# Attention's last quotient moved into the next stage, one of that stage's loads moved into attention, and one early load cut in four

## The reference

```python
def _L1_attn_ref(x, Wq, Wk, Wv, Wo):
    ...
    q = (x @ Wq.T).reshape(B, T, H, Dh)          # H = 16, Dh = 16, T = 2048
    k = (x @ Wk.T).reshape(B, T, H, Dh)
    v = (x @ Wv.T).reshape(B, T, H, Dh)
    q = _apply_rotary(q, cos, sin)
    k = _apply_rotary(k, cos, sin)
    ...
    scores = jnp.einsum('bhqd,bhkd->bhqk', q, k) * scale
    scores = jnp.where(causal[None, None], -jnp.inf, scores)
    attn = jax.nn.softmax(scores, axis=-1).astype(v.dtype)
    out = jnp.einsum('bhqk,bhkd->bhqd', attn, v)
    out = out.transpose(0, 2, 1, 3).reshape(B, T, C)
    return out @ Wo.T
...
x = L0_attn_x
x = x + _L0_attn_ref(_layernorm(x, axis=-1), ...)
x = x + _L0_ffn_ref(_layernorm(x, axis=-1), ...)
x = x + _L1_attn_ref(_layernorm(x, axis=-1), L1_attn_Wq, L1_attn_Wk, L1_attn_Wv, L1_attn_Wo)
x = x + _L1_ffn_ref(_layernorm(x, axis=-1), L1_ffn_router_w, L1_ffn_expert_weights)
```

## Time and profile before

| | us |
|---|---|
| median of 3 runs | 2865.2 (2860.91 to 2867.78) |
| the profiled execution | 2864.33 |
| its span, first to last instruction | 2862.6 |
| around the span | 1.73 |
| project_qkv | from about 1022 to 1286 |
| attention | from 1291.8 to 2319.7 |
| tail | from 2319.7 to the end |

### The profile page before, as it was taken

One profiled execution on the slowest core, in us unless ns is written; L12 is line 12 of the kernel. 1 busy time (PEld: TensorE's weight loads), 2 busy tenths in 40 slices (PEclk: granted clock), 3 DMA queues, 4 the chain that ended last, 5 costly groups with the idle time before them and its releaser, 6 DMA issues. The chain is left out here.

```text
span 2862.6 us, 63267 instructions
## 1 busy us (share of the span) xinstructions
PE 2456.2 (86%) x24666; PEld 1415.1 (49%) x24666; DVE 1570.9 (55%) x2607; ACT 1793.6 (63%) x2682; POOL 735.8 (26%) x1006
## 2 busy tenths in 40 slices
PE   6888888886688889958999999999999977789872
PEld 3555555454567656633434333333333356567652
DVE  5767768577775467745454544445554337520133
ACT  3443535343565445438999999999999933356421
POOL 2203021120000036831212111112211103464465
PEclk9999999998799899978999999999999988799986
DMA  7800000000200024575656677665667234478767
GB/s 253 274 30 2 1 1 1 1 1 9 38 1 1 1 61 145 162 136 107 112 108 115 127 115 125 113 110 102 124 123 119 48 100 150 155 259 268 257 224 238
DMA packets 251996, 308.83 MB, mean 108 GB/s; under 512 B 100544, under 2 KB 180160, under 8 KB 251584
## 3 DMA queue, kind: packets, MB, share of 16 engines
q1 hardware_dynamic: 237344, 269.49, 40.0%
q0 software_dynamic: 12288, 33.57, 3.4%
q10 hardware_dynamic: 2080, 1.84, 0.2%
HBM read 157.23 MB, written 147.59 MB: 106 GB/s over the span
## 5 line engine op out<-in xcount | busy, mean ns | idle before, releaser
L1779 ACT ACTIVATE at_PT<-at_pS 128x1024 f32<-128x1024 f32 (+2 forms) x1152 | 1002.3, 1239 | 13.7 <-PE at_pS L1806 13.6
L1634 POOL TENSOR_SCALAR_AFFINE_SELECT at_PT<-at_PT 128x256 f32<-128x256 f32 (+1 forms) x384 | 197.4, 523 | 825.3 <-ACT at_PT L1779 824.8
L1806 PE MATMUL at_pS<-hd_QT,hd_KT 99*32 99x512 bf16 (+3 forms) x5120 | 316.4, 351 | 7.4 <-DVE at_QT L1751 4.8
L1806 PE MATMUL at_pS<-at_QT,at_KT 99*32 99x512 bf16 (+3 forms) x5120 | 317.6, 349 | 2.2 <-issue 0.8
L1727 DVE COPY at_OT<-at_pO 128x512 f32<-128x512 f32 x64 | 44.3, 692 | 478.8 <-PE at_pO L1824 473.8
L1824 PE MATMUL at_pO<-at_PT,at_V 128*32 128x512 f32 (+3 forms) x2560 | 290.4, 530 | 5.8 <-issue 5.6
L1824 PE MATMUL at_pO<-at_PT,hd_V 128*32 128x512 f32 (+3 forms) x2560 | 286.7, 530 | 0.0
L2369 PE MATMUL tl_bank<-tl_W,tl_xT 128*128 x896 | 238.1, 404 | 32.0 <-issue 29.6
L1806 PEld LDWEIGHTS at_pS<-at_QT,at_KT 99*32 99x32 bf16 x5120 | 117.7, 95 | 256.2 <-ACT at_PT L1779 166.9
L1806 PEld LDWEIGHTS at_pS<-hd_QT,hd_KT 99*32 99x32 bf16 x5120 | 111.7, 95 | 267.5 <-ACT at_PT L1779 171.2
L451 ACT ACTIVATE la_ft<-la_ft 128x1024 f32<-128x1024 f32 x128 | 135.1, 1056 | 161.2 <-DVE la_ft L274 161.0
(11 more groups left out here) (353 smaller groups left out, 4161.6 us busy)
## 6 DMA issues: line engine op xcount, KB each, us to landing
tl_xin<-rows_in SPq DMA_DIRECT2D x56, 512.0 KB
rows_out<-tl_yout SPq DMA_DIRECT2D x56, 512.0 KB
score_terms<-at_parts SPq DMA_DIRECT2D x60, 384.0 KB, 5.4
rows_in<-la_zeros SPq DMA_DIRECT2D x8, 2048.0 KB, 7.6
rotated_qk<-qk_qkT SPq DMA_DIRECT2D x16, 1024.0 KB, 4.3
at_qk<-rotated_qk SPq DMA_DIRECT2D x60, 256.0 KB, 4.3
rows_in<-la_zeros SPq DMA_DIRECT2D x4, 3072.0 KB, 11.3
values<-qk_rv SPq DMA_DIRECT2D x64, 192.0 KB, 4.6
```

Source lines behind the costliest of these rows:

```text
L1634: nc.gpsimd.affine_select(out=d, in_=d, compare_op=ALU.is_ge, fill=0.0, base=0, pattern=of, channel_multiplier=-1).then_inc(masked, 1)
L1779: nc.scalar.activation(PT[u % 6][:, 0:banks, 0:width], pS[u % 3][:, 0:banks, 0:width], ACT.Exp, scale=HD ** -0.5).then_inc(exp_done, 1)
L1806: last = mm(pS[u % 3][r:r + 32, b, col:col + 512 - off], KT[par][0:KS, h, kb * P + r:kb * P + r + 32], QT[par][0:KS, h, c * 512 + off:(c + ...
```

## The change

**Attention's end.** For the last chunk of the last group (it 15, c 3) `finish` stops after the copy to `OT`. The swap, reciprocal and product are in a new function `quotient`, which DVE calls in the tail behind add(2). `keep_out(15, 3)` is left out; the four stores stand in the tail, on SP, between the weights of step c = 2 and the load of chunk 3, behind a wait for the quotient (`last_divided`). The load of chunk 15, which needs them, waits for their landing (`last_stored`). `OT` and `aT1` now lie in the buffer `y0`, which the tail first uses for its products much later.

**Attention's middle.** The load of the tail's chunk 0 is issued by SP in attention, at the end of `it` = 3, into a buffer `ay0` of its own that outlives the stage. The tail's SP starts with a semaphore increment in its place, and then loads chunk 1.

**project_qkv.** The load of `V0` is cut into four loads of 192 KB, each behind one `qkT` store of batch 2; the wait for the stores of batch 0 goes before the first.

```diff
@@ project_qkv, SP
-            store(2)
+            def first_values(q):
+                if q == 0:
+                    for f in range(4):
+                        sp.wait_ge(v_stored[f], 16 + 16 * 4)
+                sp.dma_start(keep["V0"][:, 4 * q:4 * q + 4, :], keep["v"][0, 4 * q:4 * q + 4].rearrange("t p e -> p t e")).then_inc(first_out, 16)
+            store(2, first_values)
             sp.wait_ge(first_split, 4)
             sp.dma_start(keep["terms"][0].rearrange("s r n -> r s n"), first_parts).then_inc(first_out, 16)
...
-            sp.dma_start(keep["V0"][:, :, :], keep["v"][0].rearrange("t p e -> p t e")).then_inc(first_out, 16)
             def first_terms(q):
                 if q == 0:
-                    sp.wait_ge(first_out, 32)
+                    sp.wait_ge(first_out, 80)
@@ new
+def quotient(v, dve, out, sums):
+    v.stream_shuffle(out[:, :], sums[:, :], list(range(HD, 2 * HD)) + list(range(HD)))
+    dve.drain()
+    v.reciprocal(out[:, :], out[:, :])
+    dve.drain()
+    return v.tensor_tensor(out[:, :], sums[:, :], out[:, :], ALU.mult)
@@ attention, SP
-                keep_out(it, 3)
+                if more:
+                    keep_out(it, 3)
+                if it == 3:
+                    for k in range(2):
+                        sp.wait_ge(stored[k], 64 + 2 * 128)
+                    sp.dma_start(keep["ay0"][:, :, :], keep["ao"].rearrange("(b a) h e n -> b (a h e) n", a=G)[0, :, 0:512].rearrange("(c p) n -> p c n", p=P)).then_inc(tail_loaded, 16)
@@ attention, DVE
                 v.tensor_copy(OT[:, :], pO[s][:, :]).then_inc(out_copied, 1)
...
+                if (it, c) != (NIT - 1, QC - 1):
+                    dve.drain()
+                    quotient(v, dve, aT[s], OT).then_inc(divided, 1)
@@ tail, SP
-            for c in range(NT // 4):
+            sp.sem_inc(a_loaded[0], 16)
+            for c in range(1, NT // 4):
                 if c >= 2:
                     sp.wait_ge(projected, 2 * (c - 2) + 2)
+                if c == NT // 4 - 1:
+                    sp.wait_ge(last_stored, 64)
...
+                if c == 2:
+                    sp.wait_ge(last_divided, 1)
+                    for h in range(4):
+                        sp.dma_start(keep["ao"][B * G - 1, h, :, 3 * 512:4 * 512],
+                                     keep["aT1"][32 * h + h % 2 * HD:32 * h + h % 2 * HD + HD, :]).then_inc(last_stored, 16)
@@ tail, DVE, after add(p)
+                if p == 2:
+                    quotient(v, dve, keep["aT1"], keep["OT"]).then_inc(last_divided, 1)
```

More of the change, by code:

```diff
@@ L1212, in _ @@
             store(3, first_terms)
-            sp.wait_ge(first_out, 32 + 192)
+            sp.wait_ge(first_out, 80 + 192)
             for f in range(4):
@@ L1599, in attention @@
     PT = [mem.sb(f"PT{s}", [P, 2, 512]) for s in range(6)]
-    OT = mem.sb("OT", [P, 512])
-    aT = [mem.sb(f"aT{s}", [P, 512]) for s in range(2)]
+    OT = keep["OT"]
+    aT = [mem.sb("aT0", [P, 512]), keep["aT1"]]
     scored, exp_done, masked, pv_done, out_copied, divided, split, sh_turned, sh_split, sh_out, seen = (mem.sem(n) for n in (
@@ L1719, in _ @@
             dve.sem_inc(split, 6)
-            other = list(range(HD, 2 * HD)) + list(range(HD))
             def finish(it, c):
@@ L1872, in tail @@
     Wo, R, Rc = keep["Wo"], keep["R"], mem.sb("Rc", [P, DC, E1])
-    ay = mem.sb("ay", [P, 2, DC, 512])
+    ay = [keep["ay0"], mem.sb("ay1", [P, DC, 512])]
     xT = [mem.sb(f"xT{f}", [P, 2, DC, P]) for f in range(4)]
     xin = [mem.sb(f"xin{k}", [P, NB, D]) for k in range(NX)]
-    yout = [mem.sb(f"yout{k}", [P, NB, D]) for k in range(NY)]
+    yout = [keep["y0"], mem.sb("yout1", [P, NB, D])]
     ones = mem.sb("ones", [P, P])
@@ L1928, in y_of @@
         s = t % NS_
-        return ay[:, s // 2, s % 2, k * D:(k + 1) * D]
+        return ay[s // 2][:, s % 2, k * D:(k + 1) * D]
     def wait_sent(eng, g):
@@ L2310, in project @@
                     for a in range(DC):
-                        last = mm(pP[p % 3][:, w * D:(w + 1) * D], ay[:, c % 2, a, f * P:(f + 1) * P], Wo[:, a, :], start=(a == 0), stop=(a == DC - 1))
+                        last = mm(pP[p % 3][:, w * D:(w + 1) * D], ay[c % 2][:, a, f * P:(f + 1) * P], Wo[:, a, :], start=(a == 0), stop=(a == DC - 1))
                 last.then_inc(projected, 1)
@@ L2436, in build @@
         stage("sm", soft_mixture, io, keep, st)
+        middle = Memory(nc, ctx.enter_context(ExitStack()), "md")
+        keep["ay0"], keep["y0"] = middle.sb("ay0", [P, DC, 512]), middle.sb("y0", [P, 4, D])
+        keep["OT"], keep["aT1"] = (keep["y0"][:, :, :].rearrange("p n d -> p (n d)")[:, x * 512:x * 512 + 512] for x in range(2))
         keep["qkT"] = nc.dram_tensor("rotated_qk", (B * G, P, N), fp32).ap()
```

11 lines of the change are left out of this document (4 added, 7 removed).

## The result

| | before | changed |
|---|---|---|
| median of 5 executions (us) | 2865.2 | 2844.23 |
| the profiled execution's span (us) | 2862.6 | 2842.5 |
| ratio, 95% interval | | 0.9929 (0.9913 to 0.9944) |

The changed kernel is 20.3 us faster by the ratio (16.0 to 24.9); the two medians are 21.0 apart. One of its five executions took 13596.25 us for a reason that nothing here shows, and the ratio leaves it out; the other four lie between 2842.48 and 2844.77. The forecast was 14.9 and 2850.3 us, with a range from 2845 to 2857: the direction was right, the time lies 0.8 us outside the range and 6.1 under the forecast.

What follows compares the result with a forecast made beforehand. Attention was taken as bound by ACT, project_qkv by PE, with DMA landings bounding the two changed places. Gains 12.7 (14.8 - 2.1) + 2.2 = 14.9 from 2864.33, plus 0.9 for the median: 2850.3 us, range 2845 to 2857.

Steps and rivals of the forecast that it cites:

- What is removed at the boundary: Boundary of attention and tail: without the quotient, stores and load landing, PE starts 12.55 us earlier.
- rival 3: Boundary: the barrier has a price of its own, up to 6.2 us later, 2856.5 (half of it 2853.4); chance 0.07.
- The warm start: Tail's start: PE stays at full clock, project(0) in 1.9 us; gain up to project(2) 14.8 us, 12.5 at half clock.
- Rival 1: Boundary: PE's clock falls, so the tail starts at half clock; 2852.6 us; chance 0.20.
- The price in the tail: Tail: late quotient delays turn(3) by 1.6 us and chunk 3's load delays project(6) by 0.5; 2.1 us lost.
- The load in attention and the common buffer: Attention: loading chunk 0 there, and one buffer for OT, aT1 and y0, cost 0.
- The quarters in batch 2: project_qkv, batch 2: each V0 quarter delays the first values store about 1.2 us, hidden by 2.7 us of cover; cost 0.
- Rival 5: project_qkv, batch 2: quarters delay values stores, PE stops in each quad and loses the clock; slower, 2873.9 us; chance 0.03.
- The stop in project_qkv: Behind batch 2: moving three quarters of V0 away cuts PE's idle time from 4.42 to 2.2 us; gain 2.2.
- rival 2: project_qkv stop behind batch 2: clock stays up, 2847.6 us, or the stop goes wholly, 2845.4; chance 0.15.
- DMA size: project_qkv: a 192 KB quarter, reckoned at 0.72 us, takes more than 0.95 by the skill page; gain 2.0 or less.

Runs made afterwards that it cites:

- the run with two quarters: Changed kernel with quarters 2 and 3 of V0 both behind the last qkT store, in the stop behind batch 2; ran once, 2803.63 us.

## Why the prediction was right or wrong

- **What is removed at the boundary**: right. 12.55 forecast, 12.65 in the trace; the barrier has no hidden price (rival 3 falls: 0.34 us from the copy to PE's first product).
- **The warm start**: right. project(0) takes 1.99 us in all nine traces where PE was idle for 1.17, and 3.78 where it was idle for 5.6 or more. project(2) came 4.47 us after PE's start, 4.7 forecast. Rival 1, 2852.6, did not come in any of them. The Trainium skill says that the moment of change differs between runs ("TensorE: Matmul & The Clock Gate", "What's actually happening"). The traces agree, though not at this boundary: 19 us later, ahead of project(6), a stop of 1.29 us was followed by the half clock in one trace, and stops of 1.15 to 1.25 in six others were not (last section). So rival 1 was worth its place.
- **The price in the tail**: 2.1 forecast with ends 1.6 and 2.6; measured 2.6 until project(6), the clock's 2.5 and the 0.13 by which it is late. Of its two terms the wait of turn(3) was 0.94 (forecast 1.6), and that of project(6) 1.21 (forecast 0.5, at most 1.0); the load had landed 4.6 us after its issue, where I took 3.6 to 4.5. The two idle rows give only 2.15. Without the later stores 1.6 us went, and without the quotient in one piece 0.9 more, 2.5 in all: the removal shows more than the idle rows. So the sum of the term was right to 0.5, its two parts were not.
- **The load in attention and the common buffer**: 0, as forecast, within the 0.5 us by which attention differs.
- **The quarters in batch 2**: cost 0, right. They delayed ACT by 0.6 to 1.5 us, in the 2.7 of cover. Rival 5 falls.
- **The stop in project_qkv**: the step that failed. The sentence was "I take 2.2, since the stop is still longer than the one at the boundary in which the clock began to fall". Two things were mis-sized. The first is V0's share: I took it as 2.9 us, from the landing of the terms to that of V0. Between none of V0 in the stop and the whole of it lie 3.6 us. In the same two traces, counted from the first mark, the terms land at 103.8 and 104.4: V0 shared the queues with them and held them up by 0.6 before they landed, and its own 2.9 came on top. So three quarters are worth 2.8, not 2.2, and the stop is 1.58 us, not 2.2. The second is the clock: behind a stop of 1.58 to 1.60 us it is up in all six traces that have one. That is rival 2, worth 2.75 more at the next mark (5.6 in all, forecast 4.9).

  What I set against rival 2 did not carry. The clock at 0.70 in 2312 to 2313 is some 2 us after PE's last product at 2310.42, and a stop of 2.2 lay at that edge. And the trace of the kernel before held a row that I overlooked: near 1105 PE had been idle for 2.46 us, longer than 2.2, and the same four products took 1.98, at PEclk 1.00.

```profile
1105.21 1.98 PE L1413 MATMUL qk_pQK<-fr_W,qk_zT 128*128 128x512 f32 x4 [2.46 <-ACT qk_zT L1349]
```

  Of the 5.6 some 4.4 to 5.0 arrive at attention. The loss lies behind the next stop, the one of 6.8 us: from PE's first product there to its next stop, the kernel before and then the changed one:

```profile
1237.52:1249.49 11.97, 8.25 (x28) 4.92 (x28) 4.71 (x7) 7.49 (x12) 4.73 (x6) 0.87 0.49 118
1230.63:1243.51 12.88, 9.16 (x28) 5.41 (x28) 4.71 (x7) 7.48 (x12) 4.72 (x6) 0.76 0.46 111
```

  The same 28 products take 0.9 us more, because the clock comes back later (mean PEclk 0.76 instead of 0.87). The slower products behind the stop of 3.72 (3.78 us instead of 2.48) cost nothing further, since ACT then waits for a `values` store in both kernels: the lead is 4.7 us ahead of them and 4.7 behind.
- **What is left**: of the 5.2 us between forecast and traces 2.8 are this step. 1.3 were there before any changed instruction, and 0.5 each in attention and tail, all within what executions of one kernel differ by (2860.9 to 2867.8 for the kernel before). The forecast of the median is 6.1 off and not 5.2, since I added 0.9 from the profiled execution to the median, and the changed kernel's two are equal. Rival 2 as written, 2847.6, is 3.4 off for these reasons. With this step right, or without the spread, the time would lie inside the range. The range ended at 2845 by reckoning of mechanisms alone; the spread of the runs was not in it, and it should have reached some 2 us further on either side.
- **DMA size**: from the 0.95 us that the Trainium skill gives for 64 KB ("DMA: Bandwidth & Descriptors", "Measured") I estimated over 0.95 for a quarter. Measured in the stop: 0.79 for the first, 1.19 for the second, 0.90 for a fourth of the whole V0. Most of it is there already when SP issues the terms behind the quarters: 96.00 us after the first mark with none, 96.54 with one, 97.71 with two. No run has all four quarters in the stop, so what four small loads cost against one large stays open; the gain comes from moving three of them away.

## What to carry to other kernels

Price a transfer in a full queue by taking it away: here the time between its neighbour's landing and its own (2.9 us) was less than it cost (3.6). Where a stop of TensorE is cut, ask whether the clock will still be up behind it, look through the whole trace for stops of that length and what followed them, and where both occur give both answers a like chance. And before cutting what stands in a queue, look at its order: spreading loads between the stores that somebody waits for gave 10 us here, with the same bytes.

## What the runs showed of the hardware

The clock: at the two places of the change the length of the stop and the clock behind it went together. Stops of 0.81 us (two traces), 1.17 (nine) and 1.58 to 1.60 (six) left it at 2.4 GHz; behind those of 4.39 to 4.50 (four), 5.62, 9.34 and 13.8 PE began at 1.2 GHz. But the length does not decide it alone. In the changed kernel a stop of 2.81 us left the clock at 1.00, where the one of 2.78 in the run with two quarters was followed by 0.50; in that same run the half clock followed a stop of 1.29 us ahead of project(6), which took 2.84 us instead of 1.99; and in the kernel before, the clock outlasted a stop of 4.54 us and fell 0.8 us behind it:

```profile
1103.91 1.98 PE L1413 MATMUL qk_pQK<-fr_W,qk_zT 128*128 128x512 f32 x4 [2.81 <-ACT qk_zT L1349]
```

```profile
2327.76 2.84 PE L2333 MATMUL tl_bank<-fr_W,tl_ay 128*128 128x256 f32 x8 [1.29 <-DMA tl_ay<-head_outputs]
2329.00:2330.00 1.00, 1.00 (x4) 0.73 (x4) 0.00 (x0) 0.00 (x0) 0.00 (x0) 0.50 1.01 367
```

```profile
1270.53 0.63 PE L1425 MATMUL qk_pR<-all_ident,qk_rqk 128*128 128x128 f32 x4 [4.54 <-ACT qk_qkT L1367]
1270.00:1271.00 1.00, 0.47 (x4) 0.42 (x4) 0.95 (x2) 1.00 (x3) 0.00 (x0) 1.00 0.91 94
```

Stops of 2.1 to 2.8 us near the first mark, in all thirteen traces, left the clock up. So stops between 1.3 and 4.5 us ended either way here, and no run tells what decides it.

The chips: the tail of the kernel before took 538.4 us on the first chip. On the others, of the same stage, the kernel with V0 in parts took 491.1, whose edit does not touch the tail. For the changed kernel on the first chip and on another, in the part with the experts (length, busy time of PE, PEld, DVE, ACT, POOL, then PEclk, DMA share, GB/s):

```profile
2450.00:2500.00 50.00, 29.85 (x129) 23.08 (x127) 18.79 (x53) 16.39 (x33) 33.66 (x35) 0.73 0.52 180
```

```profile
2450.00:2500.00 50.00, 47.82 (x253) 38.48 (x251) 25.32 (x83) 37.32 (x76) 38.12 (x40) 1.00 0.93 310
```

The first moves 180 GB/s where the other moves 310, with PE busy for 29.9 of 50 us instead of 47.8. Why the chips differ no run here tells; a ratio between times from two chips would say nothing of the kernels. The gain is 16.9 us (12.7 to 21.1) of 2814 there and 20.3 (16.0 to 24.9) of 2865 on the first: the intervals overlap, and the stops behind batch 2 and at the boundary are the same on both.
